# Routed experts: three of four gathered blocks turned by TensorE, one by DMA, and the loops written out

## The reference, cut to what matters

```python
x = x + xattn(layernorm(x), ctx, ctx, ...)            # x: 2 x 2048 tokens of 512
xf = layernorm(x).reshape(4096, 512)
topk_idx, w, _ = _route(xf, router_w, correction_bias) # 4 of 16 experts per token
shared_out = silu(xf @ shared_gate_w.T) * (xf @ shared_up_w.T) @ shared_down_w.T
g = einsum('sc,ech->esh', xf, gate_w)                  # H = 128
u = einsum('sc,ech->esh', xf, up_w)
hw = silu(g) * u * combine.T[:, :, None]
routed = einsum('esh,ehc->sc', hw, down_w)
x = x + shared_out + routed
```

## Time and profile before

| what | value |
|---|---|
| time, median of 3 runs | 1190.32 us (1186.72 to 1192.55) |
| the profiled execution's own time | 1181.23 us |
| its span in the profile | 1179.4 us |
| busy in the span: PE, DVE, ACT, POOL | 1035.8, 636.1, 384.6, 439.7 us |
| routed blocks, first to last matmul group | 553.5 to 961 us |

### The profile page before, as it was taken

One profiled execution on the slowest core, in us unless ns is written; L12 is line 12 of the kernel. 1 busy time (PEld: TensorE's weight loads), 2 busy tenths in 40 slices (PEclk: granted clock), 3 DMA queues, 4 the chain that ended last, 5 costly groups with the idle time before them and its releaser, 6 DMA issues.

```text
span 1179.4 us, 21927 instructions
## 1 busy us (share of the span) xinstructions
PE 1035.8 (88%) x6496; PEld 599.6 (51%) x6497; DVE 636.1 (54%) x1454; ACT 384.6 (33%) x751; POOL 439.7 (37%) x485
## 2 busy tenths in 40 slices
PE   7899499899999988886859999899988896998997
PEld 6565344444444433443636666666666652443433
DVE  4945567544443876996323434344434324784847
ACT  2423243332323634541324444344443330111111
POOL 1730320111001423324414444444444426775753
PEclk9989789999999989997979999999999998999999
DMA  9605774472537515222999989999999979975764
GB/s 347 249 23 183 192 232 112 126 222 84 156 89 197 152 58 182 82 81 63 245 197 243 252 256 235 234 250 244 247 246 250 230 223 232 394 251 178 229 176 149
DMA packets 215330, 229.64 MB, mean 195 GB/s; under 512 B 143574, under 2 KB 152568, under 8 KB 213496
## 3 DMA queue, kind: packets, MB, share of 16 engines
q1 hardware_dynamic: 191740, 151.53, 44.8%
q0 software_dynamic: 23552, 77.61, 23.6%
HBM read 124.99 MB, written 70.55 MB: 166 GB/s over the span
## 4 chain that ended last, share of the span: by engine, by line
PE 49%; DVE 17%; DMA 14%; issue 10%; ACT 4%; another core or an unknown queue 3%; POOL 1%; DVEq 1%; SPq 1%; ACTq 0%; POOLq 0%
PE bank L901 12%; PE bank L751 11%; DMA arena<-arena 6%; PE bank L920 5%; PE bank L965 4%; PE bank L767 4%; DMA arena<-xr_dram,arena 3%; PE bank L977 3%; DVE arena L1552 2%; PE bank L732 2%; DVE arena L1486 2%; PE bank L886 2%; DMA arena<-xr_dram 1%; DMA arena<-y_dram,arena 1%
## 5 line engine op out<-in xcount | busy, mean ns | idle before, releaser
L901 PE MATMUL bank<-arena 128*128 x1728 | 225.4, 280 | 44.7 <-DMA arena<-arena 22.8
L751 PE MATMUL bank<-arena 128*128 (+1 forms) x960 | 217.3, 384 | 11.7 <-DVE arena L1310 7.7
L901 PEld LDWEIGHTS bank<-arena 128*128 128x128 f16 x1728 | 165.2, 99 | 99.0 <-issue 65.3
L1672 POOL DMA_INDIRECT arena<-y_dram,arena x128 | 139.8, 1092 | 77.5 <-issue 36.3
L1651 POOL DMA_INDIRECT arena<-xr_dram,arena x144 | 141.2, 981 | 63.3 <-issue 51.6
L751 PEld LDWEIGHTS bank<-arena 128*128 128x128 f16 (+1 forms) x960 | 94.4, 99 | 129.3 <-issue 13.2
L1513 DVE SCALAR_TENSOR_TENSOR arena<-bank,arena 128x128 f32<-128x128 f32 x144 | 41.9, 291 | 189.4 <-ACT arena L1150 134.0
L965 PE MATMUL bank<-arena 128*128 128x512 f16 x576 | 131.1, 380 | 9.0 <-issue 8.7
L1087 ACT ACTIVATE arena<-arena 128x512 f16<-128x512 f32 x64 | 40.4, 631 | 252.1 <-DVE arena L1310 138.3
L920 PE MATMUL bank<-arena 128*128 x432 | 118.7, 384 | 0.3
L767 PE MATMUL bank<-arena 128*128 128x512 f16 (+1 forms) x480 | 112.7, 385 | 3.0 <-DVE arena L1312 3.0
(11 more groups left out here) (180 smaller groups left out, 1287.5 us busy)
## 6 DMA issues: line engine op xcount, KB each, us to landing
y_dram<-arena SPq DMA_DIRECT2D x144, 256.0 KB
arena<-in_x SPq DMA_DIRECT2D x8, 1024.0 KB, 12.5
xr_dram<-arena SPq DMA_DIRECT2D x16, 512.0 KB, 2.8
x_dram<-arena SPq DMA_DIRECT2D x8, 1024.0 KB, 4.7
arena<-x_dram SPq DMA_DIRECT2D x8, 1024.0 KB, 6.3
arena<-in_gu_w SPq DMA_DIRECT2D x16, 512.0 KB, 3.4
out<-arena SPq DMA_DIRECT2D x32, 256.0 KB
x1s_dram<-arena SPq DMA_DIRECT2D x5, 1024.0 KB, 5.3
```

Source lines behind the costliest of these rows:

```text
L751: last = mm(bank[g][:, :], w, xt(xv * KC + kc), start=(n == 0), stop=(n == 3 * KC - 1))
L901: last = mm(bank[2 + j][:, 0:2 * H], rows[:, r // 2, xv * KC + kc, :], only((gu_hi_r, gu_lo_r)[wp], e, slice(kc * 2 * H, (kc + 1) * 2 * H) ...
L1672: pool.indirect_dma_start(out=ybuf[n % RING][:, e, :], out_offset=None, in_=y_dram[:, :], in_offset=bass.IndirectOffsetOnAxis(ap=row_of[:, ...
```

## The change

The odd blocks with s % 4 = 1 are now turned by PE too, so 108 blocks are turned by PE and 36 by DMA. `BY_PE` lists the former and `TURN_OF` gives the number of each one's turn, by which semaphores count. `xgT_odd` has one buffer in place of two. The loops of PE, DVE, SP and POOL over the blocks are written out, with constants in the place of registers for waits and buffers; ACT's program stays a loop. The expert registers are still loaded each four blocks, now one step earlier than they are used, ahead of that step's `turn_rows`. On SP the turn of block s + 4 stands behind the write of block s, for s % 4 = 3.

```diff
+BY_PE = [n for n in range(BLOCKS) if n % 4 != 3]
+TURN_OF = {n: u for u, n in enumerate(BY_PE)}
...
-        xgT_odd = view(o1, [2, 2 * KC, P], F16)
+        xgT_odd = view(o1, [2 * KC, P], F16)
...
+            def turn_odd(s):
+
+                sp.wait_ge(s_xg[3], 16 * (s // 4 + 1))
+                if s >= 4:
+                    sp.wait_ge(s_rg, s - 3)
+                sp.dma_start_transpose(xgT_odd, xg[:, 3, :]).then_inc(s_odd, 16)
...
             sp.wait_ge(s_shl, FIRST * SH)
-            for h in range(2):
-                turn_odd(h, 16, None)
-
-            four_blocks(1)
-            x1s_out(FIRST - 1)
-            four_blocks(2)
-            later_turned_in(FIRST - 1)
-            four_blocks(3)
-            next_x1_in(FIRST - 1)
-            with sp.Fori(4, BLOCKS // 4) as i:
-                four_blocks(i)
-            for s in range(BLOCKS - 4, BLOCKS):
-                y_out(s, s % 2)
+            turn_odd(3)
+            for s in range(BLOCKS):
+                y_out(s)
+                if s % 4 == 3 and s + 4 < BLOCKS:
+                    turn_odd(s + 4)
+                if s == 3:
+                    x1s_out(FIRST - 1)
+                if s == 7:
+                    later_turned_in(FIRST - 1)
+                if s == 11:
+                    next_x1_in(FIRST - 1)
...
+            for s in range(1, BLOCKS):
+
+                n = (s - 1) % 4
+                if n == 2 and s + 2 < BLOCKS:
+                    ahead = experts(s + 1)
+                if s > 1 and s + 2 in TURN_OF:
+                    turn_rows(s + 2)
+                if s + 1 < BLOCKS:
+                    gate_up(s + 1, here[n + 2])
+                turn_h(s, s % 2, s == 1)
+                down(s - 1, n % 2, here[n], s <= 2)
+                if n == 3:
+                    here = ahead
...
+            for s in range(1, BLOCKS):
+                if s > 1 and s + 2 in TURN_OF:
+                    save_rows(s + 2)
+                if s + 1 < BLOCKS:
+                    hidden(s + 1, (s + 1) % 2, False)
+                save_h(s, s % 2, s == 1)
...
+            copy_tokens(0)
+            for s in range(BLOCKS):
+                if s >= 4:
+                    pool.wait_ge(*((s_tx, TURN_OF[s - 4] + 1) if s in TURN_OF else (s_odd, 16 * (s // 4))))
+                pool.wait_ge(s_token_now, s + 1)
+                if s + 1 < BLOCKS:
+                    copy_tokens(s + 1)
+                pool.indirect_dma_start(
+                    out=xg[:, s % 4, :], out_offset=None, in_=xr_dram[:, :],
+                    in_offset=bass.IndirectOffsetOnAxis(ap=token_now[:, s % 8:s % 8 + 1], axis=0)).then_inc(s_xg[s % 4], 16)
```

More of the change, by code:

```diff
@@ L326, in build @@
         s_tx, s_txe = sem("even_rows_turned"), sem("even_rows_turned_saved")
-        s_odd = [sem(f"odd_rows_turned{h}") for h in range(2)]
+        s_odd = sem("odd_rows_turned")
         s_rg, s_rs, s_rh = sem("routed_gate_up"), sem("routed_silu"), sem("routed_h32")
@@ L535, in _, with y_out @@
                     next_x1_in(k)
-            def y_out(s, j):
+            def y_out(s):
                 sp.wait_ge(s_ye, s + 1)
[L540 to L554, removed]
-                for h in range(2):
[L556 to L559, removed]
-            sp.wait_ge(s_shl, FIRST * SH)
-            for h in range(2):
-                turn_odd(h, 16, None)
-            four_blocks(1)
-            x1s_out(FIRST - 1)
-            four_blocks(2)
-            later_turned_in(FIRST - 1)
-            four_blocks(3)
-            next_x1_in(FIRST - 1)
-            with sp.Fori(4, BLOCKS // 4) as i:
-                four_blocks(i)
-            for s in range(BLOCKS - 4, BLOCKS):
-                y_out(s, s % 2)
+                sp.dma_start(y_tiles[s], y_sb[:, s % 2, :]).then_inc(s_yw[s % 2], 16)
+            def turn_odd(s):
[3 more added lines that the diff above has]
+                sp.dma_start_transpose(xgT_odd, xg[:, 3, :]).then_inc(s_odd, 16)
+            sp.wait_ge(s_shl, FIRST * SH)
+            turn_odd(3)
[9 more added lines that the diff above has]
+                    next_x1_in(FIRST - 1)
             sp.wait_ge(s_rd, BLOCKS)
@@ L878, in experts, with turn_rows, gate_up @@
                     skip_runtime_bounds_check_because="VectorE counts at most E - 1 experts before a block")[1]
-            def turn_rows(u, j, fresh):
-                pe.wait_ge(s_xg[2 * j], 16 * ((u >> 1) + 1))
-                if not fresh:
+            def turn_rows(s):
+                u = TURN_OF[s]
+                pe.wait_ge(s_xg[s % 4], 16 * (s // 4 + 1))
+                if u >= 2:
                     pe.wait_ge(s_txe, u - 1)
                 for n in range(2 * KC):
-                    last = turn(bank16[j][:, n * P:n * P + P], xg[:, 2 * j, n * P:n * P + P], id16)
+                    last = turn(bank16[u % 2][:, n * P:n * P + P], xg[:, s % 4, n * P:n * P + P], id16)
                 last.then_inc(s_tx, 1)
[L889 to L893, removed]
-                else:
-                    pe.wait_ge(s_txe, (s >> 1) + 1)
-                if not fresh:
+            def gate_up(s, e):
+                if s in TURN_OF:
+                    rows = xgT[:, TURN_OF[s] % 2, :, :]
+                    pe.wait_ge(s_txe, TURN_OF[s] + 1)
+                else:
+                    rows = xgT_odd
+                    pe.wait_ge(s_odd, 16 * (s // 4 + 1))
+                if s >= 2:
                     pe.wait_ge(s_rh, s - 1)
@@ L900, in gate_up @@
                     for kc in range(KC):
-                        last = mm(bank[2 + j][:, 0:2 * H], rows[:, r // 2, xv * KC + kc, :],
+                        last = mm(bank[2 + s % 2][:, 0:2 * H], rows[:, xv * KC + kc, :],
                                   only((gu_hi_r, gu_lo_r)[wp], e, slice(kc * 2 * H, (kc + 1) * 2 * H)),
@@ L922, in down @@
                 last.then_inc(s_rd, 1)
[L924 to L928, removed]
-            turn_h(0, 0, True)
[L930 to L952, removed]
+            here, ahead = experts(0), None
+            turn_rows(0)
+            gate_up(0, here[0])
+            turn_rows(1)
+            gate_up(1, here[1])
+            turn_rows(2)
+            turn_h(0, 0, True)
+            for s in range(1, BLOCKS):
[10 more added lines that the diff above has]
+                    here = ahead
+            down(BLOCKS - 1, 1, here[3], False)
             def gate_up_at(n):
@@ L1491, in _, with save_rows @@
             shared_sum(WITH + 1)
-            def save_rows(u, j, fresh):
+            def save_rows(s):
+                u = TURN_OF[s]
                 dve.wait_ge(s_tx, u + 1)
-                if not fresh:
-                    dve.wait_ge(s_rg, 2 * u - 3)
-                V.tensor_copy(xgT[:, j, :, :], bank16[j].rearrange("p (n q) -> p n q", n=2 * KC)).then_inc(s_txe, 1)
+                if u >= 2:
+                    dve.wait_ge(s_rg, BY_PE[u - 2] + 1)
+                V.tensor_copy(xgT[:, u % 2, :, :], bank16[u % 2].rearrange("p (n q) -> p n q", n=2 * KC)).then_inc(s_txe, 1)
             def save_h(s, j, fresh):
@@ L1516, in hidden @@
                 V.tensor_tensor(r_hb[:, j, 1, :], r_h[:, j, :], r_hb[:, j, 0, :], ALU.subtract).then_inc(s_rhl, 1)
-            save_rows(0, 0, True)
-            save_rows(1, 1, True)
+            save_rows(0)
+            save_rows(1)
             hidden(0, 0, True)
+            save_rows(2)
             hidden(1, 1, True)
             save_h(0, 0, True)
[L1523 to L1534, removed]
+            for s in range(1, BLOCKS):
[4 more added lines that the diff above has]
+                save_h(s, s % 2, s == 1)
             def combine(n):
@@ L1636, in _, with copy_tokens @@
             pool.wait_ge(s_tok, 1)
[L1638 to L1647, removed]
+            def copy_tokens(s):
+                pool.tensor_copy(token_now[:, s % 8:s % 8 + 1], token_of[:, s:s + 1]).then_inc(s_token_now, 1)
+            copy_tokens(0)
+            for s in range(BLOCKS):
+                if s >= 4:
+                    pool.wait_ge(*((s_tx, TURN_OF[s - 4] + 1) if s in TURN_OF else (s_odd, 16 * (s // 4))))
                 pool.wait_ge(s_token_now, s + 1)
-                if not last:
-                    copy_tokens(s + 1, (r + 1) % 8)
+                if s + 1 < BLOCKS:
+                    copy_tokens(s + 1)
                 pool.indirect_dma_start(
[L1652 to L1662, removed]
+                    out=xg[:, s % 4, :], out_offset=None, in_=xr_dram[:, :],
+                    in_offset=bass.IndirectOffsetOnAxis(ap=token_now[:, s % 8:s % 8 + 1], axis=0)).then_inc(s_xg[s % 4], 16)
             for j in range(2):
```

## The result

The changed kernel takes 1256.55 us (median; 1253.43 to 1261.46) against 1190.32: **1.061 times the time before, 95% interval 1.055 to 1.066**. The profiled execution took 1255.52 us of its own, 74.3 more than before's 1181.23.

The account below looks back on a forecast made before the run. PE was taken to set the pace before; afterwards, waits for DMA turns behind SP's writes. 35 cycles at 13.8 instead of 10.70 us add 108, the start gives 5 back: 1190 + 103 = 1293 us, range 1238 to 1354.

Parts of the forecast that it names:

- TensorE sets the pace before: Routed blocks, kernel before: PE sets the pace, four blocks take 10.70 us, only 4.3 us of DMA waits in 300.
- 36 more turns on PE, 16.2 us; DVE hidden: PE's 36 extra turns at 0.45 us add 16.2 us to the path; DVE's 36 extra copies, 24.6 us, are hidden.
- The order on SP decides: Turn issued at T (end of `down`) + 1.6, landing 3.5 us later; PE waits 2.6 us in every four blocks.
- The cycle: Four blocks on PE, from one DMA-turned block's `gate_up` to the next: 13.0 us, 13.8 with the clock's loss, against 10.70.
- the register load and seam: Loading eight expert registers at the loop's seam on PE: 0.68 us kept in four blocks, ends 0 and 0.85.
- Rival D: Writing out pays more: all issue idle on PE goes, 24 us less, 1269 us; chance 0.08.
- The clock: PE's clock falls to its lower level behind somewhat under half the waits: 0.75 us a cycle, ends 0 and 1.7.
- The start of the stage: First 86 us of the routed blocks, where 22 us are lost: fewer DMA turns give 5 us back, from 0 to all.
- The sum: 35 waits at 13.8 - 10.70 us give +108, less 5 at the start: +103 us, 1293 us.
- The band: Whole kernel's time: own forecast 1262 to 1325 us at chance 0.50; full range 1238 to 1354 us.
- rival A: The wait for turns stays short, 2.3 us with 3.2 to landing, clock full: 1238 to 1260 us; chance 0.18.
- Rival C: The DMA turn is hidden behind PE's work: four blocks take 10.3 us, 1154 us in all; chance 0.05.

Follow-up runs that it names:

- the mended order: The changed kernel with only SP's order changed: the DMA turn of block n stands behind the write of block n - 6, not n - 4; ratio 0.986, 1144.59 us.
- the repeat: The changed kernel run once more, unchanged, on the chip of its variants; 1.059 times the kernel before.
- Filling: The changed kernel with throw-away transposes of a constant on PE ahead of each wait for a DMA turn; ratio 1.061 with 24, 1.050 with 12.

## Why the prediction was right, point by point

- *TensorE sets the pace before*: right as the rows stand, with 4.3 us of waits for turns in 300, but by less than it seemed. With PE's loop alone written out, 16 us of PE's own time went and 18 us of waits for turns came: the DMA turns were close behind. Where only one block in four is turned by DMA and the order is mended, the cycle is 9.62 us, the sum of PE's steps.
- *36 more turns on PE, 16.2 us; DVE hidden*: right. One turn more in each cycle, from the mended order (9.62 us) to all turned by PE (10.06), costs 0.44 us. The changed kernel's DVE copies are 108 of 0.68 us, and `gate_up` waited for them three times, 2.5 us in all.
- *The order on SP decides, a wait in each of 35 cycles*: right, 35 waits. Put at 2.6 us, measured 2.2: T to issue was 1.38 us (1.6 forecast), landing as forecast (3.5).
- *The cycle*: 13.8 forecast, 13.19 measured. The step that was mis-sized is the register load and seam, 0.68 us kept, 0 measured: up to T a cycle with the clock up takes 7.28 us, not 7.9. 0 was one of the ends that I had given it; the nearest row mixed the loop's own work with the load. Rival D had this right. The load itself is 0.59 us and lies under the queued work:
```profile
L865 PEldq TENSOR_LOAD <-arena x36: 587/591/1262, 548.7 to 1011.2; - x36
```
  That is 74 ns for each of eight registers, where the Trainium skill ("Runtime: NRT & Kernel Launch", section "Instruction fetch mechanics") has about 200; the load here reads from the arena in SBUF, and whether that makes the difference no run shows. The preference for written-out programs that the Trainium skill states in the same section held for the seam, and not for the whole, as the run with PE's loop alone written out shows.
- *The clock*: 0.75 us forecast, 1.0 measured, and 0.73 in the repeat (8.01 - 7.28). The falls came after shorter waits than the 2.44 us of the earlier trace rows, from 1.84 on. Filling gave about 0.55 us of the repeat's 0.73 back; four falls were left.
- *The start of the stage*: 5 us back forecast; the first five cycles took 64.6 us and 72.7 before, though the longer cycle is in them, 5 x 2.5 us, so about 20 us came back, nearly all of the 22 that were lost there.
- *The sum*: 103 us forecast, 66 measured at the median. The stage grew by 69.4: its first five cycles are 8 us shorter, the other 30 and the edges 77 longer, of which 30 x (13.19 - 10.70) are 75. Of the 34 us that the stage falls short of the forecast about half is the cycle, 30 x (13.8 - 13.19) = 18, and about half the start. The 9 us between the profiled execution and the median did not carry over either: between profiled executions the difference is 74 us, between medians 66.
- *The band*: the 1256.55 us lie under my own 1262 to 1325 and inside rival A's 1238 to 1260. What A tells did not happen, though: the landing took 3.5 us and not 3.2, and the clock fell 19 times. The time came out there by the seam, the start and the 9 us, so that it fits A is luck.
- *Rival C*, hidden turns, is what the mended order gives, at the price of two blocks' lead. Its gain, a ratio of 0.986, is less than the 0.970 that 1154 us would be.

What I had at nothing and is not: writing out PE's program, which costs where two of four blocks are turned by DMA (1.3 to 1.8%). With one of four the DMA share is 0.87 with the order mended and PE waits for turns for only 6.2 us; whether a kernel with one of four in loops would be faster still no run shows.

## What to carry to other kernels

A DMA in an in-order queue is only as early as what stands ahead of it. When loops are rewritten, compare for each transfer the block it is for with the block of the wait ahead of it, before and after: here 6 became 4, and it outweighed all else that changed. Price a transfer's landing beside what will be in flight when it is issued, not by its best case. And a resource that falls from 94% to 64% busy need not be a gain: here it was the sign of a cycle bound by a chain of handovers.

## What the runs showed of the hardware

- A DMA transpose of 128 x 1024 numbers of 16 bits landed 2.8 to 4.8 us after its issue, 3.4 on average, in the changed kernel, where the last gather had been issued at least 2.8 us before; and 4.7 us at the least, 5.4 on average, with the turn behind the write of block n - 5, where a gather had been issued 0.06 to 0.5 us before.
- In the changed kernel PE's granted clock fell to its lower level at waits from 1.84 us up, not at each of them (19 falls in 24 waits), and never behind those of 1.6 us or less; 0.67 us of throw-away transposes in each wait cut the falls from 17 to 4.
- A written-out program of PE (the kernel before with PE's loop alone written out) fetched 16 KB about each 12.6 us in the steady part; the same work in a loop fetched nothing from 640 to 940 us.
